# Moving the softmax exponential one slot later on ScalarE, in a fused attention and mixture-of-experts kernel

## The chip, the cores and the metric

The kernel runs on one core of a Trainium2 chip, in one launch. The metric is device time in microseconds (us): the median of three runs, and for the trace one profiled execution with its own time.

## The reference, cut to what matters

For 16 graphs of 512 nodes with 256 features, a masked attention with 8 heads of 32 is followed by a gate, and then by a mixture of 8 experts, top 2, with one shared expert. The change touches only the attention's softmax:

```python
q = (x @ Wq.T).reshape(b, n, NH, DK)          # b = 16, n = 512, NH = 8, DK = 32
k = (x @ Wk.T).reshape(b, n, NH, DK)
v = (x @ Wv.T).reshape(b, n, NH, DK)
scores = jnp.einsum('bqhd,bkhd->bhqk', q, k) / jnp.sqrt(jnp.float32(DK))
scores = jnp.where((adj != 0)[:, None, :, :], scores, -jnp.inf)
attn = jax.nn.softmax(scores, axis=-1)
c = jnp.einsum('bhqk,bkhd->bqhd', attn, v).reshape(b, n, h)
gate = jax.nn.sigmoid(jnp.concatenate([c, x], axis=2) @ Wg.T + bg)
return gate * x + (1.0 - gate) * c
```

x is layer-normalised before it, and the expert part comes after it on the sum of x and this result.

## The kernel before, in words

**Slots.** A batch is one graph. Its 8 heads times 4 tiles of 128 queries are 32 tiles of scores, each 128 x 512, and each tile has a slot p = 0 to 31 of the batch. Every engine walks the slots in the same order, written out in the program for all batches; the engines meet only at semaphores. A tile goes through a pipeline, and each step lags the score by a fixed number of slots, the constants at lines 82 to 86:

- TensorE in slot p: the score of tile p (L480); then four transposes of tile p - 3 (`TURN = 3`, L490), which first wait for the exponential of that tile (`p_exp`, L486) and for the copy of tile p - 5, whose PSUM bank they reuse (`t_free`, L488); then the slot's unit of other work; then, in slots 4, 12, 20 and 28, the product of P and V for 8 tiles (L511, 32 matmuls).
- VectorE in slot p: adds the mask to score p, scales, writes it to `pf` in SBUF and takes the row extreme `nmax` (L836, `s_done`); then the parts that belong to units.
- ScalarE in slot p: first it evacuates the unit that TensorE finished in slot p - 1 (L540 to L559); then it copies the transposed tile p - 4 out of PSUM (`EVAC = 4`, L597, `t_free`); then it takes the exponential of tile p - 1 (`EXP = 1`, L609), in place in `pf` with the row sums as accumulator output, which needs `s_done` of tile p - 1 and gives `p_exp`. Each exponential is two instructions, the ACTIVATE and the read of the accumulator. The copy is ahead of the exponential in each slot.

`pf` is a ring of 8 tiles, the scores have two PSUM banks, and the transposed tiles two.

**Units.** `UNIT_AT` (L24) puts the other work of a batch in slots: projections for the next batch (Q0 in slots 22 and 23, K0 in 24 and 25), for this one (Q1, K1, V0, V1 in 2 to 9), transposes (P0, P1, C0, C1, X0, X1), the gate (Z0 to Z3 in 14 to 17) and the router (L0, M0, R0 in 0, 1 and 12). A unit reaches VectorE for the low half after ScalarE has evacuated its high half.

**Head loads.** The query and key rows of a head are restacked by three DMAs from `qk` to `stack` (L303). SyncE issues those of heads 0 to 3 of the next batch, 12 in a row, once VectorE has the low half of K0 (L700). Score p of slots 0 to 3 needs head p there.

**Scatter.** From slot 17 GpSimd sends 8 indirect DMAs (L923) of the batch before to the experts' buffer.

After the 16th batch the engines pass to the experts' part (L1320 and on), of which only the beginning overlaps the attention.

Of the kernel before, what the change touches and what calls it, by code (L numbers as in the profile page):

```python
# [65 lines left out]
def attention_phase(nc, sems, held, banks, x, adj, wqkv, wgate, bg, router_w, xn_dram, x1_dram, xt2_dram, xg_dram,  # L66
# [13 lines left out]
    SCALE = float(DK) ** -0.5  # L80
    E = router_w.shape[1]
    TURN = 3
    EXP = 1
    EVAC = 4
    PV = 12
    BACK = 21
# [6 lines left out]
    if True:  # L93
# [187 lines left out]
        def behind(b, p, lag, att):  # L281

            if p >= lag:
                return b, p - lag, att
            before = att if not isinstance(b, int) else 0 < b <= NB
            return b - 1, p - lag + POS, before
# [239 lines left out]
        def scalar(act):  # L526
# [40 lines left out]
            def at(b, p):  # L567
# [22 lines left out]
                if was:  # L590
# [3 lines left out]
                    if ep % TB_ == 0 and (not isinstance(eb, int) or eb > 0 or ep >= 16):  # L594
# [4 lines left out]
                                   ACT.Copy).then_inc(t_free, 1)  # L599
                eb, ep, was = behind(b, p, EXP, att)  # L600
                if was:
# [1092 lines left out]
def program(nc, x, adj, wqkv, wgate, bg, router_w, w_all, out):  # L1694
# [12 lines left out]
    with ExitStack() as ctx:  # L1707
# [11 lines left out]
        with ExitStack() as held:  # L1719
            att = attention_phase(nc, ctx, held, banks, x, adj, wqkv, wgate, bg, router_w, xn_dram, x1_dram, xt2_dram,  # L1720
                                  xg_dram, ident, msum, xn2, idx, s_scat, region)
# [85 lines left out]
```

## Time and profile before

| | |
|---|---|
| median of 3 runs | 1925.34 us (1923.04 to 1927.98) |
| profiled execution, its own time | 1923.95 us |
| its span, first to last instruction | 1922.2 us |
| TensorE busy over the span | 1765.3 us (92%) |
| VectorE busy | 1274.3 us (66%) |
| ScalarE busy | 1104.5 us (57%) |
| 512 exponentials (L609), without the accumulator reads | 371.8 us |
| 512 copies of transposed tiles (L597) | 304.9 us |
| chain that ended last, share by engine | PE 42%, issue 1%, DMA 1% |

Times are read from the span's start. PE is TensorE's matmul side, PEld its weight loads (which the same sequencer issues, and which overlap the matmuls), DVE is VectorE, ACT is ScalarE, POOL is GpSimd, SP is SyncE. Idle time before an instruction is put down to what ended it. The clock column gives the granted TensorE clock as a share of full speed. The chain that ended last is traced only from 1034 us on, so that for the attention the timelines are read instead.

### The profile page before, as it was taken

How to read it: one execution, taken by the hardware profiler on the slowest of the kernel's cores; microseconds unless marked ns; L12 is line 12 of the kernel's file. 1: busy time of each engine (PE TensorE's matmuls, PEld its weight loads, DVE VectorE, ACT ScalarE, POOL GpSimd, SP SyncE). 2: the span in 40 equal slices, each digit the busy share in tenths (PEclk: the TensorE clock that was granted, in tenths of full speed). 3: DMA queues.
4: the chain of work that ended last, by engine and by line, in shares of the span. 5: the costliest groups of instructions: out<-in, count | busy, mean ns of one | idle time of the engine just before them, and what ended most of it. 6: DMA issues, size and time to landing. Idle time of an engine off the chain costs nothing. (4 is left out here: it accounts for less than half of the span.)

```text
span 1922.2 us, 36029 instructions
## 1 busy us (share of the span) xinstructions
PE 1765.3 (92%) x12613; PEld 1468.7 (76%) x12613; DVE 1274.3 (66%) x3155; ACT 1104.5 (57%) x2509; POOL 672.8 (35%) x512
## 2 busy tenths in 40 slices
PE   5899999988999888999889996989999999999996
PEld 4677777667777667777577885878989898898986
DVE  5676666766767766766645552467777777777773
ACT  4888778877778877778623331324444444444342
POOL 0125534335534335443221133003434343443334
PEclk8999999999999999999889996999999999999999
DMA  5445455544455544455213343245656565555553
GB/s 151 133 135 143 130 165 158 151 133 136 133 168 156 148 142 128 138 166 165 100 56 121 104 148 113 90 157 150 174 144 168 148 176 144 166 154 163 156 154 39
DMA packets 141329, 269.19 MB, mean 140 GB/s; under 512 B 15456, under 2 KB 92640, under 8 KB 136160
## 3 DMA queue, kind: packets, MB, share of 16 engines
q1 hardware_dynamic: 112608, 226.19, 38.3%
q0 software_dynamic: 28128, 39.93, 9.8%
q8 instruction: 102, 1.67, 0.4%
q10 hardware_dynamic: 416, 0.79, 0.2%
q14 instruction: 75, 0.61, 0.1%
HBM read 141.99 MB, written 74.52 MB: 113 GB/s over the span
## 5 line engine op out<-in xcount | busy, mean ns | idle before, releaser
L836 DVE CUSTOM_DVE_ANT_0 pf<-bank,bias_q 128x512 f32<-128x512 f32 x512 | 348.3, 687 | 268.6 <-PE bank L480 238.5
L1196 POOL DMA_INDIRECT out_x<-yb,ix x142 | 245.5, 1729 | 498.8 <-ACT yb L1414 408.0
L609 ACT ACTIVATE pf<-pf,nmax 128x512 f32<-128x512 f32 x512 | 371.8, 726 | 49.5 <-DVE nmax L836 49.5
L1426 ACT ACTIVATE ah<-am 128x512 fp32r<-128x512 f32 (+1 forms) x220 | 133.1, 605 | 440.8 <-DVE am L1494 434.8
L490 PE MATMUL bank<-ident,pf 128*128 128x128 f32 x2048 | 315.1, 276 | 55.5 <-issue 29.2
L1327 PE MATMUL bank<-xh,wl 128*128 128x512 f32 (+1 forms) x880 | 336.1, 382 | 6.0 <-issue 6.0
L490 PEld LDWEIGHTS bank<-ident,pf 128*128 128x128 f32 x2048 | 252.6, 142 | 115.3 <-issue 68.2
L1325 PE MATMUL bank<-xh,wh 128*128 128x512 f32 (+1 forms) x880 | 337.6, 384 | 3.2 <-issue 2.3
L1326 PE MATMUL bank<-xl,wh 128*128 128x512 f32 (+1 forms) x880 | 336.0, 382 | 2.0 <-issue 1.9
L597 ACT ACTIVATE pt<-bank 128x512 f32<-128x512 f32 x512 | 304.9, 596 | 13.9 <-PE bank L490 13.8
L480 PE MATMUL bank<-stack 96*128 96x512 f32 x512 | 237.2, 464 | 35.2 <-DMA stack<-qk 18.0
L1497 DVE TENSOR_TENSOR al<-am,ah 128x512 fp32r<-128x512 f32 (+1 forms) x220 | 146.7, 667 | 147.6 <-ACT ah L1426 144.8
L1325 PE MATMUL bank<-wh,ah 128*128 128x256 f32 x824 | 236.3, 287 | 3.5 <-issue 3.5
L1327 PE MATMUL bank<-wh,al 128*128 128x256 f32 x824 | 233.6, 283 | 3.6 <-issue 3.5
L1326 PE MATMUL bank<-wl,ah 128*128 128x256 f32 x824 | 233.2, 283 | 1.7 <-issue 1.7
L1494 DVE TENSOR_TENSOR am<-sg,bank 128x512 f32<-128x512 f32 (+1 forms) x220 | 143.0, 650 | 110.1 <-PE bank L1327 104.3
L1327 PEld LDWEIGHTS bank<-xh,wl 128*128 128x128 f32 x880 | 167.2, 190 | 39.3 <-issue 6.4
L1325 PEld LDWEIGHTS bank<-xh,wh 128*128 128x128 f32 x880 | 167.6, 190 | 38.3 <-issue 8.0
L1424 ACT ACTIVATE sg<-bank 128x512 f32<-128x512 f32 (+1 forms) x220 | 124.5, 566 | 121.0 <-PE bank L1327 88.8
L1326 PEld LDWEIGHTS bank<-xl,wh 128*128 128x128 f32 x880 | 167.7, 191 | 33.1 <-issue 2.6
L923 POOL DMA_INDIRECT xg_dram<-xn,idx x128 | 129.6, 1012 | 119.5 <-DVE idx L820 76.6
L480 PEld LDWEIGHTS bank<-stack 96*128 96x128 f32 x512 | 98.0, 192 | 88.8 <-issue 36.7
(213 smaller groups left out, 3202.3 us busy)
## 6 DMA issues: line engine op xcount, KB each, us to landing
raw<-in_w_all SPq DMA_DIRECT2D x39, 1536.0 KB, 7.3
stack<-qk SPq DMA_DIRECT2D x378, 128.0 KB, 2.4
xb<-xg_dram SPq DMA_DIRECT2D x32, 520.0 KB
adj_i<-in_adj SPq DMA_DIRECT2D x32, 512.0 KB, 5.1
xn<-in_x SPq DMA_DIRECT2D x16, 512.0 KB, 6.3
xn_dram<-xn SPq DMA_DIRECT2D x16, 512.0 KB
xp<-in_x SPq DMA_DIRECT2D x16, 512.0 KB, 6.7
xnp<-xn_dram SPq DMA_DIRECT2D x16, 512.0 KB, 7.6
```

The costliest lines, as they stand in the source:

```text
L480: pe.matmul(S[p % 2][:, :], stack[0:SR, hd, 0, P * tq:P * tq + P], stack[0:SR, hd, 1, :], start=True, stop=True).then_inc(s_full, 1)
L490: last = pe.transpose(T[ep % 2][:, P * kt:P * kt + P], pf[ep % RING][:, P * kt:P * kt + P], ident[:, :])
L597: act.activation(pt[r][:, j, :, P * (tq % 2):P * (tq % 2) + P], T[ep % 2][:, :].rearrange("p (k q) -> p k q", q=P), ACT.Copy).then_inc(t_f ...
L609: act.activation(pf[i][:, :], pf[i][:, :], ACT.Exp, bias=nmax[:, i:i + 1], scale=-1.0, accum_out=den[:, g, tq, j:j + 1]).then_inc(p_exp, 1)
L836: dve.tensor_tensor_reduce(pf[r][:, :], S[p % 2][:, :], bias_q[1 - par][:, tq, :], -SCALE, -3.0 * MASKED, ALU.add, ALU.min, nmax[:, r:r + ...
L1196: pool.indirect_dma_start(out=out, out_offset=bass.IndirectOffsetOnAxis(ap=ix[n % RING][:, i:i + 1], axis=0), in_=yb[s][:, i, :], in_offse ...
L1325: pe.matmul(out_, lh, rh, start=first, stop=False)
L1326: pe.matmul(out_, lh, rl, start=False, stop=False)
L1327: return pe.matmul(out_, ll, rh, start=False, stop=last)
L1426: act.activation(ah[s][:, m, 0:cols], am[m % 2][:, 0:cols], ACT.Copy).then_inc(s_ah, 1)
L1494: dve.tensor_tensor(am[m % 2][:, 0:cols], sg[m % 2][:, 0:cols], UB[m % 2][:, 0:cols], ALU.mult).then_inc(s_am, 1)
L1497: dve.tensor_tensor(al[s][:, m, 0:cols], am[m % 2][:, 0:cols], f32(ah[s][:, m, 0:cols]), ALU.subtract).then_inc(s_al, 1)
```

## The change

ScalarE takes the exponential of tile p - 2 in slot p, in place of that of tile p - 1. Nothing else is moved: the copy keeps its lag of 4, the transposes theirs of 3. The number of instructions and their sizes stay as they are; the last exponential of a batch now falls in slot 1 of the next one.

```diff
@@ -80,7 +80,7 @@
     SCALE = float(DK) ** -0.5
     E = router_w.shape[1]
     TURN = 3
-    EXP = 1
+    EXP = 2
     EVAC = 4
     PV = 12
     BACK = 21
```

## Rows read from the trace of the kernel before

**Rows 1.** Windows, attention: busy PE, PEld, DVE, ACT, POOL; clock, DMA share, GB/s

```profile
26.00:950.00 924.00, 834.99 (x7059) 650.23 (x7059) 633.27 (x1999) 736.72 (x1797) 364.38 (x292) 0.97 0.50 143
```

**Rows 2.** Waits, 240 to 890 us: who waited for whom, us, times, longest

```profile
ACT pf L609 <- DVE nmax L836: 26.6, 43, 1.2
...
PE bank L490 <- ACT pt L597: 18.8, 45, 0.7
...
PEld bank L480 <- DMA stack<-qk: 11.8, 17, 1.4
...
PE bank L480 <- DMA stack<-qk: 6.0, 11, 1.0
```

**Rows 3.** Timeline of ScalarE, slots 24 to 30: start, us, instruction, idle before

```profile
522.56 0.20 ACT L609 ACTIVATION_READ_ACCUMULATOR pf<-pf,nmax 128x1 f32 x1
...
523.50 0.73 ACT L609 ACTIVATE pf<-pf,nmax 128x512 f32<-128x512 f32 x1 [0.25 <-DVE nmax L836]
...
524.23 0.57 ACT L546 ACTIVATE qk<-bank 128x512 fp32r<-128x512 f32 x1
...
525.88 0.59 ACT L597 ACTIVATE pt<-bank 128x512 f32<-128x512 f32 x1
...
526.97 0.20 ACT L609 ACTIVATION_READ_ACCUMULATOR pf<-pf,nmax 128x1 f32 x1
...
530.01 0.60 ACT L597 ACTIVATE pt<-bank 128x512 f32<-128x512 f32 x1 [0.46 <-PE bank L490]
```

**Rows 4.** Timeline of TensorE's weight loads, slots 25 and 28

```profile
522.18 0.57 PEld L490 LDWEIGHTS bank<-ident,pf 128*128 128x128 f32 x4
...
526.59 0.42 PEld L490 LDWEIGHTS bank<-ident,pf 128*128 128x128 f32 x4 [0.61 <-ACT pf L609]
```

**Rows 5.** Timeline of TensorE's weight loads, slots 0 to 2 of the next batch

```profile
532.07 0.57 PEld L490 LDWEIGHTS bank<-ident,pf 128*128 128x128 f32 x4
...
534.80 0.47 PEld L490 LDWEIGHTS bank<-ident,pf 128*128 128x128 f32 x4
```

**Rows 6.** Timeline of ScalarE, slots 31 to 1

```profile
532.30 0.19 ACT L609 ACTIVATION_READ_ACCUMULATOR pf<-pf,nmax 128x1 f32 x1
...
533.92 0.28 ACT L556 ACTIVATE lgt<-bank 128x128 f32<-128x128 f32 x1 [0.24 <-PE bank L452]
...
535.18 0.20 ACT L609 ACTIVATION_READ_ACCUMULATOR pf<-pf,nmax 128x1 f32 x1
```

**Rows 7.** Timeline of TensorE: K0's last matmul in slot 25, z matmuls in slot 0

```profile
523.29 0.40 PE L396 MATMUL bank<-xt_h,wqkv_l 128*128 128x512 f32 x1
...
533.43 0.43 PE L452 MATMUL bank<-z,rw_wide 128*32 128x128 f32 x8 [0.20 <-DVE z L713]
```

**Rows 8.** Timeline of SyncE's queue: the loads of heads 0 to 3

```profile
526.53 7.98 SPq L303 DMA_DIRECT2D stack<-qk  x12
```

**Rows 9.** Timeline of ScalarE, slot 10

```profile
550.45 0.73 ACT L609 ACTIVATE pf<-pf,nmax 128x512 f32<-128x512 f32 x1 [1.22 <-DVE nmax L836]
```

**Rows 10.** Timeline of TensorE's weight loads, slots 11 and 12

```profile
550.47 0.19 PEld L480 LDWEIGHTS bank<-stack 96*128 96x128 f32 x1 [0.78 <-DVE nmax L836]
...
551.58 0.19 PEld L480 LDWEIGHTS bank<-stack 96*128 96x128 f32 x1
552.35 0.42 PEld L490 LDWEIGHTS bank<-ident,pf 128*128 128x128 f32 x4 [0.58 <-issue]
```

**Rows 11.** Timeline of TensorE, slots 20 and 28

```profile
512.72 0.63 PE L490 MATMUL bank<-ident,pf 128*128 128x128 f32 x4 [2.52 <-issue]
513.27 3.62 PE L511 MATMUL bank<-pt,v 128*32 128x256 f32 x32
...
527.17 1.93 PE L511 MATMUL bank<-pt,v 128*32 128x256 f32 x32
```

**Rows 12.** Timeline of GpSimd's scatter, the last of 8 DMAs

```profile
512.04 0.96 POOL L923 DMA_INDIRECT xg_dram<-xn,idx  x1 [0.30 <-issue]
```

**Rows 13.** Windows, the product of slot 20: columns as in the first group

```profile
514.00:516.00 2.00, 2.00 (x24) 1.05 (x20) 1.38 (x4) 1.60 (x4) 0.00 (x0) 0.50 0.00 0
```

## The prediction, made before the change was run

> **What bounds the kernel now.** I began with the busy time by stretch. In the 924 us of attention TensorE is busy 835 us and ScalarE 737 us [rows 1]: near enough that each paces some slots. The table of waits says where they meet: ScalarE's exponentials wait for VectorE 43 times, 26.6 us in all, which is what the change goes for; and TensorE's transposes wait for ScalarE's copies 45 times, 18.8 us, which is what it may worsen [rows 2]. The chain of waits does not reach back to the attention, so I then went through the timelines of one batch (500 to 558 us) slot by slot; the other batches repeat it to some hundredths, except in slots 0 to 3 and at both ends.
>
> The key reading is the distance between a copy on ScalarE and the transposes that reuse its bank. The copy that starts at 525.88 ends at 526.47, and the next transposes' weight load starts at 526.59, 0.12 us later [rows 3, 4]. TensorE stands there and goes as soon as the copy is out. (The page names L609 as releaser; that exponential had long been done, it is the copy.)
>
> **What the change does to the order.** Transposes of slot p need the exponential of tile p - 3. Before, ScalarE takes it in its slot p - 2; with the change it is the last thing of slot p - 1, behind the very copy that TensorE already waits for. No instruction is added. The wait of TensorE in slot p is now for the end of ScalarE's slot p - 1. The exponential that stands there in the trace tells when: its accumulator read ends at 526.97 + 0.20 = 527.17, so the load that started at 526.59 starts at 527.28 or later, 0.69 us late [rows 3, 4]. What was queued behind it on TensorE is the unit of the slot, or the product of P and V, then the next score, for which VectorE waits.
>
> In the other direction ScalarE gains: its 43 waits for `nmax` go, since that tile is a slot older.
>
> **Where the delay counts.** Only where ScalarE or VectorE later wait for TensorE.
>
> *Slots 25 to 29.* ScalarE is the pacer from 524.23 on, without a gap, to 529.5. In slot 25 the transposes start at 522.18, and ScalarE's slot before ends at 522.76; plus 0.11 that is 0.69 late. K0's last matmul, which ends at 523.69 now, then ends at 524.38, and K0's evacuation, at 524.23 now, follows at about 524.4: +0.2. ScalarE's wait of 0.25 in that slot vanishes, but the evacuation is then held by TensorE, so the gain is not kept [rows 3, 4, 7]. Then ScalarE runs its slots at its own pace, and the transposes of slot 28 come 0.69 + 0.2 = 0.89 late. Behind them is the product of P and V, 1.93 us [rows 11], after which TensorE is the pacer: ScalarE's copy in slot 30 waits 0.46 us for it already [rows 3]. So the whole 0.89 us lands on ScalarE.
>
> *Slot 0.* The transposes start at 532.07, ScalarE's slot ends at 532.49, plus 0.11: 0.53 late, on top. Then come the z matmuls, of which the second half waits 0.20 us for VectorE, which absorbs that much; the evacuation of L0 already waits 0.24 us for them. Net +0.34 [rows 5 to 7].
>
> *Slot 2.* Start 534.80, ScalarE's end 535.38, plus 0.11: 0.69, call it 0.70 late, ahead of Q1 and the score of slot 3 [rows 5, 6]. Sum from slot 25 to slot 3: 0.89 + 0.34 + 0.70 = 1.93 us.
>
> *What absorbs part of it.* The score of slot 3 waits for head 3's load. The 12 loads leave SyncE's queue one after the other in 7.98 us from the low half of K0 on [rows 8], so they shift only by about 0.2 us, and TensorE, coming later, waits less. Over the twelve batches from 240 us these waits total 6.0 us on the matmul side and 11.8 us on the load side [rows 2]: 0.50 to 0.98 us a batch. I take 0.70, since a part of a load's wait is the ordinary spacing. Net 1.93 - 0.70 = 1.23 us a batch, 14.8 us in twelve. The three seams before them have longer waits for the loads, so I give them 2.0 us together.
>
> *Slots 7 to 11.* Transposes 0.0 to 0.2 us late, but VectorE paces here: the score of slot 11 waits for it, 0.78 us at the load [rows 10]. Cover is enough; uncovered it would be 0.2 us a batch, 3 us.
>
> *Slot 12, the gain.* ScalarE waits 1.22 us for `nmax` in slot 10 [rows 9], and for that reason its slot 11 copy is late and the transposes of slot 12 wait 0.58 us. That load starts at 552.35, so the copy ended at about 552.24; ScalarE's slot 11, exponential included, ends 0.70 us after its copy, and without the wait 1.22 us sooner: 551.7, before TensorE comes. TensorE is then held by its own order only. Of the 0.77 us from the score's load to the transposes' (551.58 to 552.35), the load itself takes 0.19 and the wait 0.58; some 0.2 of idle stays at a score ahead of transposes, so about 0.39 us is gained [rows 10], at most 0.39 x 13 = 5.1 us. I take it as nothing for all batches with a scatter: TensorE stands in slots 18 to 20 while the 8 scatter DMAs go out (2.52 us before the transposes of slot 20; last issue 512.04) [rows 11, 12], and the scatter hangs on VectorE's variance in slot 12, which is not moved. It comes to the same stretch a little earlier and waits more.
>
> *Slots 19 and 20.* Both transposes would be 0.69 late, but in the same stand. I take nothing, and keep 0.69 x 12 = 8.3 us as the upper bound. Slots 14 to 18 are paced by the gate's matmuls; nothing.
>
> *First batches.* No scatter yet: two product slots come late, two gain in slot 12: +0.3 us.
>
> *The end.* The experts' part starts behind the last batch and is passed on whole.
>
> **Sum.** 14.8 + 2.0 + 0.3 = 17.1 us. Against the profiled execution's own 1923.95 us (span 1922.2) that is 1941.0; that execution is 1.4 us under the median of the runs, so 1941 to 1942.4. I predict 1941, 0.8% slower. Downward: the full gain of slot 12 (-5.1) and the larger absorption (-0.28 x 12 = -3.4): 1932.5. Upward: the smaller absorption (+2.4) and slots 19 and 20 (+8.3): 1951.7.
>
> **The clock.** Slot 20's product runs at a granted clock of 0.50 (1.2 of 2.4 GHz) after the stand of 2.52 us, and takes 3.62 us, where that of slot 28 takes 1.93 us [rows 11, 13]. The change widens the wait ahead of the transposes of slot 28 from 0.61 to some 1.3 us, and that of slot 27 likewise. Should the clock fall there as well, each batch pays up to 3.62 - 1.93 = 1.69 us more. In this batch only the longer stand was followed by a fall, so this is a rival and no term. The Trainium skill, "TensorE: Matmul & The Clock Gate", Part 1 ("The HAM clock gate") says that an idle TensorE is throttled to half its clock and activity releases it, and Part 4 ("PE-mode transpose") that transposes do not count as activity in the same way, which speaks against a change that leaves little but transposes and waits there. By that rule the time would be that of the clock rival below; by the row of slot 28's product, 1.93 us behind a wait of 0.61 us and transposes, it is not [rows 4, 11].
>
> **The rivals.**
> - *Slower, as summed:* 1941, own range 1932 to 1952. Chance 0.80 (with slots 19 and 20 in it).
> - *Hidden:* the head loads are the real pacer of each seam, and the transposes' delay only eats into their wait. Each seam then costs the 0.2 us of K0: 15 x 0.2 = 3 us, 1927. It decides where the wait for loads is above 1.9 us in each batch; the longest is 1.4 [rows 2]. Chance 0.10.
> - *Faster:* ScalarE freed of its 26.6 us of waits runs ahead, and its earlier copies let TensorE start the slots after 10 sooner: 15 x 0.39 = 5.9 us, 1918. It needs ScalarE's slot to end before TensorE comes in slots 25, 0 and 2 too, where it now ends 0.4 to 0.6 us after. Chance 0.05.
> - *Clock:* 1941 + 14 x 1.69 = 1965. Chance 0.05.
>
> A measurement of this kernel tells about 0.3% (6 us) from no change. Faster by more: 0.04; within: 0.11; slower: 0.85. Range for eight times in ten: 1931 to 1952.
>
> **What the profile after would show.** Right: the transposes' wait for L609 or the issue in slots 2, 12 (smaller), 19, 20, 25, 27 and 28, each load starting 0.11 us behind an accumulator read and not behind a copy; the exponentials' waits for `nmax` nearly gone; slots 29 to 29 of the next batch 58 to 60 us apart, with nearly no wait for `stack`; slots 14 to 18 unchanged. Wrong: a granted clock of 0.5 near slot 28 (clock); the load wait still there in slot 3 (hidden); slots 12 to 21 shorter by 0.4 us (gain kept) or longer (slots 19 and 20 count). The weakest steps are the stand in slots 18 to 20, which I take as given from outside without knowing its cause, and the mean of 0.70 for the head loads.

## The result, and the profile after

The changed kernel took 1941.93 us in the median of 11 runs (1934.48 to 1948.19), the kernel before 1925.61 us in 11 runs beside it (1923.04 to 1932.9). The ratio is 1.0074, with a 95% interval of 1.0057 to 1.0091: slower by 0.74%. Its profiled execution took 1940.37 us with a span of 1938.6 us; before these were 1923.95 and 1922.2.

The groups of instructions on the page after, with busy time, mean ns of one, and idle time before them:

```profile
L836 DVE CUSTOM_DVE_ANT_0 pf<-bank,bias_q 128x512 f32<-128x512 f32 x512 | 349.0, 687 | 280.5 <-PE bank L480 251.2
...
L490 PE MATMUL bank<-ident,pf 128*128 128x128 f32 x2048 | 323.4, 281 | 74.9 <-ACT pf L609 40.3
...
L609 ACT ACTIVATE pf<-pf,nmax 128x512 f32<-128x512 f32 x512 | 371.3, 725 | 9.4 <-DVE nmax L836 9.4
L490 PEld LDWEIGHTS bank<-ident,pf 128*128 128x128 f32 x2048 | 250.1, 143 | 149.8 <-ACT pf L609 78.4
...
L597 ACT ACTIVATE pt<-bank 128x512 f32<-128x512 f32 x512 | 305.0, 596 | 37.6 <-PE bank L490 37.3
```

The exponentials hardly wait any more (9.4 us left in the whole span, 49.5 us before). In their place the transposes' weight loads stand 78.4 us behind the exponential, and ScalarE's copies stand 37.3 us behind TensorE (13.8 us before). No instruction became slower: 725 ns for an exponential, 596 ns for a copy. The waits of the same stretch as [rows 2], 240 to 890 us (who waited for whom, us in all, times, longest):

```profile
PEld bank L490 <- ACT pf L609: 51.1, 70, 1.3
...
PE bank L490 <- ACT pf L609: 26.6, 56, 1.0
...
ACT qk L546 <- PE bank L396: 24.3, 44, 0.9
ACT pt L597 <- PE bank L490: 23.5, 29, 1.1
...
PE bank L490 <- ACT pt L597: 4.9, 3, 1.8
...
PEld bank L480 <- DMA stack<-qk: 3.4, 8, 0.7
```

The wait that the change goes for, ScalarE's for `nmax` (43 times before), is gone from the list; that of the transposes for the copies fell from 45 times to 3; and the loads' wait for the heads' DMAs fell from 11.8 to 3.4 us, since TensorE comes later. The first row is what grew. Before the change it read:

```profile
PEld bank L490 <- ACT pf L609: 7.3, 12, 0.6
```

One seam, batch 9 into batch 10, with ScalarE in slots 24 to 30 and then 0 to 2, to be laid beside [rows 3, 6]:

```profile
591.19 0.60 ACT L546 ACTIVATE qk<-bank 128x512 fp32r<-128x512 f32 x1 [0.25 <-PE bank L396]
...
592.78 0.20 ACT L609 ACTIVATION_READ_ACCUMULATOR pf<-pf,nmax 128x1 f32 x1
...
593.96 0.20 ACT L609 ACTIVATION_READ_ACCUMULATOR pf<-pf,nmax 128x1 f32 x1
...
597.64 0.60 ACT L597 ACTIVATE pt<-bank 128x512 f32<-128x512 f32 x1 [1.10 <-PE bank L490]
...
602.82 0.20 ACT L609 ACTIVATION_READ_ACCUMULATOR pf<-pf,nmax 128x1 f32 x1
```

And TensorE's weight loads in the same stretch, to be laid beside [rows 4, 5]: slots 25, 27 and 28, then 0, the z matmuls, and 2; the last two are the score's and the transposes' of slot 12, to be laid beside [rows 10].

```profile
589.81 0.42 PEld L490 LDWEIGHTS bank<-ident,pf 128*128 128x128 f32 x4 [0.70 <-ACT pf L609]
...
593.03 0.42 PEld L490 LDWEIGHTS bank<-ident,pf 128*128 128x128 f32 x4 [1.28 <-ACT pf L609]
...
594.22 0.42 PEld L490 LDWEIGHTS bank<-ident,pf 128*128 128x128 f32 x4 [0.61 <-ACT pf L609]
...
600.17 0.42 PEld L490 LDWEIGHTS bank<-ident,pf 128*128 128x128 f32 x4 [0.42 <-ACT pf L609]
600.76 0.46 PEld L452 LDWEIGHTS bank<-z,rw_wide 128*32 128x32 f32 x16 [0.17 <-issue]
...
603.07 0.42 PEld L490 LDWEIGHTS bank<-ident,pf 128*128 128x128 f32 x4 [0.69 <-ACT pf L609]
...
619.37 0.19 PEld L480 LDWEIGHTS bank<-stack 96*128 96x128 f32 x1
619.62 0.46 PEld L490 LDWEIGHTS bank<-ident,pf 128*128 128x128 f32 x4
```

Read the two together. The accumulator read that starts at 592.78 ends at 592.98, and the load goes at 593.03; the next ends at 594.16, the load goes at 594.22; the one of slot 1 ends at 603.02, the load of slot 2 goes at 603.07. Each load goes 0.05 or 0.06 us behind the end of ScalarE's whole slot, where before it went 0.12 us behind the copy [rows 3, 4]. In slot 12 the transposes' load follows the score's after 0.25 us without a wait, where it took 0.77.

**Where the 16.4 us of span went.** The start of each score (L480) marks the slots. I took its distance from the score before over batches 3 to 14, and give the means in us:

| slots | before | after | |
|---|---|---|---|
| 0 to 5 | 9.62 | 9.56 | -0.06 |
| 5 to 12 | 10.43 | 10.42 | 0 |
| 12 to 13 | 3.53 | 3.05 | -0.48 |
| 13 to 18 | 9.61 | 9.62 | 0 |
| 18 to 21 | 9.53 | 10.15 | +0.62 |
| 21 to 24 | 4.06 | 4.27 | +0.21 |
| 24 to 29 | 8.32 | 8.90 | +0.58 |
| 29 to 0 | 2.92 | 2.92 | 0 |
| batch | 58.02 | 58.88 | +0.86 |

Twelve batches make 10.36 us (12 x 0.863). Up to the first score of batch 3 it is 186.83 - 183.36 = 3.47 us, in the last batch 1.36 us, behind its last score 1.23 us; the sum is 16.42 us. Of the 3.47 us, 2.6 lie in batch 0, and 0.94 lie ahead of the very first score (at 26.97 us after, 26.03 before), where no exponential has run yet: that part is not the change's. The first score starts at 25.1 to 27.0 us in all the kernels of this document.

### The profile page after: what moved, and what is told of

It is laid out like the page before. It is cut to its first block and busy times, and to the rows that moved or that the text cites. A ratio compares the mean times of both kernels' runs of the same rounds, so it can differ in the third digit from the quotient of the medians.

```text
span 1938.6 us, 36029 instructions
## 1 busy us (share of the span) xinstructions
PE 1772.6 (91%) x12613; PEld 1469.6 (76%) x12613; DVE 1281.5 (66%) x3155; ACT 1105.2 (57%) x2509; POOL 672.0 (35%) x512
## 5 line engine op out<-in xcount | busy, mean ns | idle before, releaser
L490 PE MATMUL bank<-ident,pf 128*128 128x128 f32 x2048 | 323.4, 281 | 74.9 <-ACT pf L609 40.3
L609 ACT ACTIVATE pf<-pf,nmax 128x512 f32<-128x512 f32 x512 | 371.3, 725 | 9.4 <-DVE nmax L836 9.4
L490 PEld LDWEIGHTS bank<-ident,pf 128*128 128x128 f32 x2048 | 250.1, 143 | 149.8 <-ACT pf L609 78.4
L597 ACT ACTIVATE pt<-bank 128x512 f32<-128x512 f32 x512 | 305.0, 596 | 37.6 <-PE bank L490 37.3
L480 PE MATMUL bank<-stack 96*128 96x512 f32 x512 | 235.5, 460 | 26.4 <-DVE nmax L836 11.5
L1325 PEld LDWEIGHTS bank<-wh,ah 128*128 128x128 f32 x824 | 156.1, 189 | 6.1 <-issue 5.6
```

Of the source, the lines that this page charges most:

```text
L480: pe.matmul(S[p % 2][:, :], stack[0:SR, hd, 0, P * tq:P * tq + P], stack[0:SR, hd, 1, :], start=True, stop=True).then_inc(s_full, 1)
L490: last = pe.transpose(T[ep % 2][:, P * kt:P * kt + P], pf[ep % RING][:, P * kt:P * kt + P], ident[:, :])
L597: act.activation(pt[r][:, j, :, P * (tq % 2):P * (tq % 2) + P], T[ep % 2][:, :].rearrange("p (k q) -> p k q", q=P), ACT.Copy).then_inc(t_f ...
L609: act.activation(pf[i][:, :], pf[i][:, :], ACT.Exp, bias=nmax[:, i:i + 1], scale=-1.0, accum_out=den[:, g, tq, j:j + 1]).then_inc(p_exp, 1)
L1325: pe.matmul(out_, lh, rh, start=first, stop=False)
```

## The experiments

Every kernel here computes all that the kernel before does. The kernel before was timed again beside each.

**Order against lag (two runs).** In both, ScalarE's exponential stands ahead of its copy in each slot; the first keeps the old lag, the second takes the new one.

```diff
-                eb, ep, was = behind(b, p, EVAC, att)
...
                 eb, ep, was = behind(b, p, EXP, att)
...
+                eb, ep, was = behind(b, p, EVAC, att)
```

> The exponential keeps its lag of one slot, but stands ahead of the copy in ScalarE's slot. Theory (what costs is that the transposes wait for the end of ScalarE's previous slot, whichever instruction stands there): the transposes of slots 25, 27, 28, 2, 19 and 20 start 0.11 us behind the end of a copy that now stands last, some 0.5 to 0.7 us later than before, and slots 24 to 29 take about 8.9 us in place of 8.26. The waits for nmax stay (26.6 us between 240 and 890 us). Time 1935 to 1950 us. Rival (the greater age of the exponential is what costs, the order in a slot is nothing): 1925 us, slots 24 to 29 at 8.26.

> The exponential two slots behind, as in the changed kernel, and ahead of the copy. Theory (end of the slot counts): the two orders are alike, since the transposes need both the exponential and the copy of the same slot of ScalarE; slots 24 to 29 at 8.8 to 8.9 us, time 1937 to 1946 us. Rival (it is the exponential's place behind the copy that costs): the transposes' waits fall back to the 0.61 us of before, 1925 us or below, since the waits for nmax are gone too.

Lag 1: 1947.55 us, ratio 1.0109 (1.0087 to 1.0132). Lag 2: 1945.21 us, ratio 1.0102 (1.0082 to 1.0121). Both times are in the ranges expected; slots 24 to 29 are somewhat longer than expected, 9.38 us with lag 1 and 9.03 with lag 2. With lag 2 the transposes wait for a copy that now ends ScalarE's slot, and the product of slot 28 starts 7.17 us behind the score of slot 24, as against 7.03 after the change and 6.39 before. So it doesn't matter much which of the two instructions is last: TensorE needs both, and what costs is that it needs the end of the slot. (This order is, if anything, some 0.3% slower than the change; the two intervals overlap a little.) With lag 1 the exponential's wait for `nmax` also holds the copy behind it, which is the other way to lose. Slots 5 to 12 take 11.53 us there, before 10.43. ScalarE in the exponential-first kernel with lag 1, in slots 29 and 30:

```profile
597.28 0.60 ACT L608 ACTIVATE pt<-bank 128x512 f32<-128x512 f32 x1
599.53 0.72 ACT L598 ACTIVATE pf<-pf,nmax 128x512 f32<-128x512 f32 x1 [1.64 <-DVE nmax L836]
600.16 0.19 ACT L598 ACTIVATION_READ_ACCUMULATOR pf<-pf,nmax 128x1 f32 x1
600.25 0.57 ACT L608 ACTIVATE pt<-bank 128x512 f32<-128x512 f32 x1
```

**All of the pipeline one slot later.** If the cost is only that TensorE needs the end of ScalarE's slot, then moving the transposes, the copies and the product too should leave the gain alone.

```diff
-    TURN = 3
-    EXP = 1
-    EVAC = 4
-    PV = 12
-    BACK = 21
+    TURN = 4
+    EXP = 2
+    EVAC = 5
+    PV = 13
+    BACK = 22
```

(`SEAM_HEAD`, the number of slots at a batch's head that still belong to the batch before, goes from 4 to 6.)

> Exponential, transposes, copy, product and the evacuation of the product all one slot later (2, 4, 5, 13, 22), and the first expert step two slots later so that the last tiles are out of its banks. Theory: the distance from exponential to transposes is back, so no transposes wait for an accumulator read; slots 24 to 29 at 8.26 us or near, slots 0 to 3 back to a floor of 4.10, and the gain of slot 12 (0.4 to 0.5 us a batch) is kept or lost in the stand of slots 18 to 20. 1918 to 1927 us. Rival (the later exponentials cost in another way, through the masked scores' ring or the row sums): 1935 us or more.

It took 1968.78 us, ratio 1.0208 (1.0185 to 1.0232): a plain miss. The products land in slots 5, 13, 21 and 29, beside other units than before, and a batch takes 61.15 us: slots 21 to 24, with the product of slot 21 among them, take 11.08 us (before 4.06), while slots 18 to 21 take 5.71 (before 9.53). That is not the stall of slots 18 to 20 moving away. TensorE in slots 20 and 21 of batch 9 of that kernel:

```profile
590.13 0.63 PE L490 MATMUL bank<-ident,pf 128*128 128x128 f32 x4 [2.53 <-issue]
590.51 0.48 PE L480 MATMUL bank<-stack 96*128 96x512 f32 x1
593.07 1.09 PE L490 MATMUL bank<-ident,pf 128*128 128x128 f32 x4 [2.08 <-ACT pt L597]
594.09 3.64 PE L511 MATMUL bank<-pt,v 128*32 128x256 f32 x32
```

It stands 2.53 us in slot 20, as before (2.52), and then another 2.08 us in slot 21. ScalarE shows why: its evacuations of P0 and P1 come late here as they do before (idle 2.04 and 1.16 us ahead of them, before 2.04 and 1.14), but before, the product of slot 20 runs while the second is late and covers it. With the product one slot on, the second stand is bare, and the product behind it still takes 3.64 us. Slots 18 to 24 take 16.79 us, before 13.59: 3.20 us a batch, or 38 of the 42 us lost. The run says nothing for or against the reason under test, as it changes what stands beside what.

**The delays taken back one group at a time.** A constant `LATE` lists the tiles whose exponential comes two slots behind; the others keep one. A tile's transposes follow in the third slot behind it.

```diff
-    EXP = 1
+    LATE = (8, 9, 10)
...
-                eb, ep, was = behind(b, p, EXP, att)
-                if was:
+                for lag in (2, 1):
+                    eb, ep, was = behind(b, p, lag, att)
+                    if not was or (ep in LATE) != (lag == 2):
+                        continue
```

Those are the tiles of the gain in slot 12 alone. The other three keep lag 2 for all tiles but those whose transposes fall in slots 24 to 29, in slots 31 to 2, or in slots 18 to 21.

> Only the exponentials of tiles 8, 9 and 10 of each batch are taken two slots behind, all others one. Theory: slot 12's transposes no longer wait, slots 12 to 13 take about 3.05 us in place of 3.53, no other stretch but the stand of slots 18 to 21 is touched. If the stand swallows it, 1925 us; if it is kept, 1925.6 - 0.48 x 13 = 1919 us. I expect it to be swallowed: 1923 to 1926.

> As the changed kernel (two behind), but tiles 21 to 26 of each batch, whose transposes fall in slots 24 to 29, one behind as before. Theory: slots 24 to 29 fall from 8.90 back to 8.3 us, the floor of slots 0 to 3 stays at 4.68, slots 12 to 13 stay at 3.05; 0.6 x 15 = 9 us less than the changed kernel, 1933 us, if the stand of slots 18 to 21 is as in the changed kernel. Rival (the loss of the changed kernel is in the stand alone): 1942 us.

> As the changed kernel, but tiles 28 to 31 of each batch, whose transposes fall in slots 31 to 2, one behind as before. Theory (the head loads absorb what is late here): the floor of slots 0 to 3 falls from 4.68 to 4.10 us, and the waits for the loads come back, so that the mean of slots 0 to 3 stays near 4.5 to 4.8; the time moves by -4 us at most, 1938 to 1942. Rival (the loads absorb nothing): -0.58 x 15 = -9 us, 1933.

> As the changed kernel, but tiles 15 to 18 of each batch, whose transposes fall in slots 18 to 21, one behind as before. Theory A (the stand got 0.8 us longer because its transposes are dispatched later): slots 18 to 24 fall from 14.4 to about 13.6 us and the time to 1931. Theory B (it got longer because TensorE comes to it 0.48 us earlier relative to the scatter): they stay at 14.4 or scatter from batch to batch as now, 1940 to 1943. In batches 0 and 1, which have no scatter, slots 18 to 21 lose 0.3 to 0.6 us in both.

| late tiles | us | ratio (interval) | slots 0-3 | 12-13 | 18-24 | 24-29 | batch |
|---|---|---|---|---|---|---|---|
| none (before) | 1925.6 | 1 | 4.82 | 3.53 | 13.59 | 8.32 | 58.02 |
| all (after) | 1941.93 | 1.0074 (1.0057 to 1.0091) | 4.80 | 3.05 | 14.42 | 8.90 | 58.88 |
| 8 to 10 | 1924.45 | 0.9994 (0.9982 to 1.0007) | 4.91 | 3.05 | 13.16 | 8.55 | 57.49 |
| not for 24 to 29 | 1935.99 | 1.0038 (1.0015 to 1.0060) | 5.03 | 3.05 | 14.20 | 8.18 | 58.20 |
| not for 31 to 2 | 1937.86 | 1.0057 (1.0034 to 1.0080) | 4.70 | 3.05 | 14.65 | 8.90 | 59.06 |
| not for 18 to 21 | 1931.74 | 1.0027 (1.0013 to 1.0041) | 4.77 | 3.05 | 14.05 | 8.90 | 58.48 |

The slot columns are means of batches 3 to 14 in one profiled execution. Three things follow.

First, slots 24 to 29: with the old lag there they are back at 8.18, from 8.90, and the time falls by 0.36% (1.0074 to 1.0038; the two intervals just overlap). It was this delay that lengthened them. But the waits for the heads come back, 4.80 to 5.03 in slots 0 to 3. Second, slots 31 to 2: taking the delay back there gives 0.10 us in slots 0 to 3 and a fall of the ratio by 0.17%, which its interval doesn't tell from nothing. The head loads had absorbed that delay. Third, slots 18 to 21: taking the delay back there gives 0.47%, 1.0074 to 1.0027. The two intervals don't meet. (That it gives more than slots 24 to 29 do is not shown.) Its trace shows less of it than its time: slots 18 to 24 take 14.05 us, which is 0.37 less than after the change and 0.46 more than before, but its profiled execution was the slowest of its ten (1936.67 us).

The gain of slot 12 by itself is there in every batch, 3.53 to 3.05 us, but with it alone the time is 0.9994 of that before, which is no measured gain: 12 x 0.48 = 5.8 us would be 0.30%, and the interval ends at 0.18%. So at least part of it is lost again behind slot 12. The profiled execution of that kernel was the fastest of its 12 (1916.04 us), so its batch of 57.49 us flatters it.

**The stall in slots 18 to 20.** I had taken it as given, without its cause. In the next runs the scatter's 8 DMAs are held until VectorE is in slot 20 of the batch, with lag 1, with lag 2, and with the three late tiles; in the last they are let go one per slot from slot 17 on, with lag 1.

```diff
+                    if A + 2 < NB:
+                        pool.wait_ge(s_done, (A + 2) * POS + 20)
```

```diff
+                if A + 2 < NB:
+                    pool.wait_ge(s_done, (A + 2) * POS + 17 + j)
```

> The kernel before (exponentials one behind), with GpSimd's scatter held until the score of slot 19 is masked, some 5 us later than it would start. Theory (the stand is tied to the scatter, not to the slots): P0 and P1 are evacuated 1.66 and 3.3 us after the score of slot 18, as in batch 1, slots 18 to 21 take 5.3 to 6 us, and a stand appears in slots 21 to 26 in their place; its sum decides the time, 1900 to 1935. Rival (the stand belongs to slots 18 to 20, scatter or not): slots 18 to 21 stay at 9.5 us, 1925.

> All exponentials two behind, with the scatter held until the score of slot 19 is masked, to be read against the same with one behind (1925 us). Slots 18 to 21 are then free of the stand in both. Theory (late transposes in slots 19 and 20 cost when no stand covers them): slots 18 to 21 take 5.31 + 0.65 = 5.95 us, slots 12 to 13 3.05 in place of 3.53, the floor of slots 0 to 3 4.7 in place of 4.1, and in slots 24 to 29, where the stand now is, from nothing to 0.64 more. Sum per batch -0.48 + 0.65 + 0.58 + (0 to 0.64) = 0.75 to 1.4 us, 1935 to 1944 us. Rival (the changed kernel is slow only because its stand is longer): 1925 us or below.

> Tiles 8 to 10 two behind, the rest one, and the scatter held as in the run before with one behind. Theory (the gain of slot 12 is kept, since the scatter now hangs on the score of slot 19, which comes earlier too): slots 12 to 13 at 3.05, nothing else changed, 1925 - 0.48 x 14 = 1918 us. Rival (what is gained ahead of the scatter is given back in its stand wherever it is): 1925 us.

> The kernel before, with the eight scatter DMAs of a batch sent one per slot, held until the scores of slots 16 to 23 are masked, in place of one after the other. Theory A (the stand is caused by each DMA, or by the bytes): its sum is the same, spread over slots 18 to 26, 1925 us. Theory B (it comes from their following each other closely): slots 18 to 21 fall to 5.3 to 6 us and the later ones stay, up to 4.3 x 12 = 50 us less, 1875 us. Slots with transposes and late evacuations show which.

Held, with lag 1: 1924.92 us, ratio 0.9985 (0.9971 to 1.0). Slots 18 to 21 fall from 9.53 to 5.31 us, and slots 24 to 29 rise from 8.32 to 13.44: the stall went with the scatter, at full size, and so gained nothing. GpSimd's DMA issues of that kernel in batch 9, the second and the last:

```profile
573.75 1.92 POOL L925 DMA_INDIRECT xg_dram<-xn,idx  x1 [0.30 <-issue]
...
582.33 0.96 POOL L925 DMA_INDIRECT xg_dram<-xn,idx  x1 [0.30 <-issue]
```

TensorE, from K0's last matmul in slot 25 on (the second line is the score of slot 27, the third the transposes of slot 27, the last the product of slot 28):

```profile
580.71 0.40 PE L396 MATMUL bank<-xt_h,wqkv_l 128*128 128x512 f32 x1
...
581.62 0.48 PE L480 MATMUL bank<-stack 96*128 96x512 f32 x1
585.81 1.09 PE L490 MATMUL bank<-ident,pf 128*128 128x128 f32 x4 [3.70 <-ACT pt L597]
...
588.11 3.59 PE L511 MATMUL bank<-pt,v 128*32 128x256 f32 x32
```

and ScalarE's evacuation of that K0:

```profile
584.58 0.60 ACT L546 ACTIVATE qk<-bank 128x512 fp32r<-128x512 f32 x1 [2.85 <-remote]
```

Read the three in order of time. The last DMA issue ends at 583.29. K0's last matmul had ended at 581.11, and ScalarE had nothing else to do from 581.73 on, yet it begins K0's evacuation at 584.58, 3.5 us behind the matmul; its wait is put down to no instruction ("remote"). The copy behind it comes late, and so TensorE stands 3.70 us. The product then takes 3.59 us, much as that of slot 20 does before [rows 11]; the half clock costs 3.59 - 1.93 = 1.66 us, and moves with the stall.

The three others ran on another chip, where the kernel before takes 1836.92 us in 13 runs (1833.02 to 1841.12), 4.6% less than on the chips of all runs above. They can be compared with that time only. Held, lag 2: 1870.09 us, ratio 1.0177 (1.0155 to 1.02). Held, three tiles late: 1872.0 us, 1.0187 (1.0161 to 1.0213). Spread, lag 1: 1841.08 us, 1.0021 (1.0009 to 1.0033).

| kernel | 0-3 | 12-13 | 18-21 | 24-29 | 29-31 | batch |
|---|---|---|---|---|---|---|
| held, all tiles late | 4.68 | 3.05 | 5.95 | 8.90 | 3.76 | 55.71 |
| held, three tiles late | 4.22 | 3.05 | 5.31 | 8.28 | 5.74 | 56.33 |
| spread, no tile late | 4.68 | 3.53 | 5.31 | 8.28 | 2.45 | 53.80 |

None of the three has the stall, though the two held ones send their 8 DMAs as closely as the first held kernel did, which had it at full size. In the spread kernel of that table TensorE's transposes and product of slot 20 go like this, though DMAs of the scatter are issued at 540.93, 542.20 and 544.04 us:

```profile
542.23 0.63 PE L490 MATMUL bank<-ident,pf 128*128 128x128 f32 x4 [0.27 <-ACT pt L597]
542.79 1.93 PE L511 MATMUL bank<-pt,v 128*32 128x256 f32 x32
```

Here the change's own terms can be read without it: +0.64 in slots 18 to 21 (5.95 against 5.31), +0.62 in slots 24 to 29, -0.48 in slot 12. What the two held kernels lose is something else: the transposes of the next batch's rows (slots 29 and 30) wait for GpSimd, which normalises them behind the held scatter. The waits of the held kernel with all tiles late, 240 to 890 us:

```profile
PE bank L400 <- POOL xn L966: 14.5, 11, 1.6
```

In the held kernel on the other chip slots 29 to 31 take 2.24 us as before; there the stall ahead of them seems to give GpSimd the time.

The profile of the kernel before was not taken on the faster chip, so that it has no stall there is argued, but on good grounds. Its time is 4.6% less, and the spread kernel, whose time is within 0.3% of it, has none in its trace. And the experts' part, which is the same code in all kernels, has a second train of indirect DMAs, 32 in a row from L1178 (a line or two later in some kernels). The 60 us from the first of them on, in the columns of [rows 1], first in the kernel before and then in the spread kernel:

```profile
1132.00:1192.00 60.00, 42.16 (x186) 33.05 (x185) 19.63 (x42) 11.81 (x20) 31.80 (x32) 0.74 0.43 141
```

```profile
1075.00:1135.00 60.00, 60.00 (x333) 52.24 (x332) 31.59 (x60) 20.97 (x35) 32.02 (x32) 1.00 0.60 194
```

TensorE stands 17.6 us around them in the first, at a mean clock of 0.74, and not at all in the second. It is so in every trace: 17.6 to 22.4 us in the eleven of the slower chips, none in the three of the faster one. From the first of these DMAs to the end of the span it is 790.2 to 794.3 us there and 764.3 to 765.0 here. Since the train is not spread in the spread kernel either, it is the chip that makes this difference. Whether spreading the scatter would remove the stall on the other chips stays open.

One kernel had lost most of the stall already, on a slower chip and with the scatter untouched: the exponential ahead of the copy, lag 1. Its slots 18 to 21 take 6.01 us in eight batches of the twelve (before 9.5 to 9.8 in eleven). TensorE's P0 and ScalarE's evacuation of it, first before, then in batch 9 of that kernel:

```profile
507.73 0.60 PE L400 MATMUL bank<-ident,xn 128*128 128x128 f32 x4
...
511.49 0.60 ACT L540 ACTIVATE xt_h<-bank 128x512 fp32r<-128x512 f32 x1 [2.04 <-remote]
```

```profile
578.20 0.60 PE L400 MATMUL bank<-ident,xn 128*128 128x128 f32 x4
...
579.19 0.60 ACT L540 ACTIVATE xt_h<-bank 128x512 fp32r<-128x512 f32 x1
...
581.67 1.93 PE L511 MATMUL bank<-pt,v 128*32 128x256 f32 x32
```

The evacuation starts 3.16 us behind the matmuls before, and 0.39 us behind them here, and the product of slot 20 (the last line) runs at full speed. Yet the scatter is issued around all of this, from 573.15 to 584.74 us. So the scatter beside these slots is not enough for the stall. What the order of ScalarE's two instructions has to do with it, no run tells. The kernel is still slower than before, by what its exponentials' waits cost elsewhere (slots 5 to 12 +1.10 us, 24 to 29 +1.06, 29 to 0 +0.36).

**The change once more.** The last run was the changed kernel itself.

> The changed kernel itself, once more, in the hope of a chip on which the kernel before takes 1837 us. The kernel before took 1926 to 1927 us on two chips and 1837 us on a third. My theory: what the change costs by its order (0.64 us in slots 25 to 29, 0.58 us in slots 0 to 2 less 0.59 us that the head loads absorb, 0.48 us won in slot 12) is the same on each chip, and what happens in slots 18 to 24 is not. Where the kernel before takes about 1926 us I expect a ratio of 1.007 again and slots 18 to 21 at 9.5 to 10.5 us. Where it takes about 1837 us I expect slots 18 to 21 at 5.3 to 6.0 us, slots 24 to 29 at 8.90, and 14 to 20 us more than before, 1.008 to 1.011. Rival, that the cost is mostly the stand's: there no more than 6 us, 1.003.

It fell on a chip where the kernel before takes 1927.04 us: 1940.45 us (1938.02 to 1945.27), ratio 1.0078 (1.0063 to 1.0094), with slots 18 to 21 at 10.11 us, 24 to 29 at 8.90 and slot 12 at 3.05. The result was got a second time, and the question it was sent for was not answered.

## Why the prediction was right, and where it was not

The time, 1941 forecast and 1941.93 measured, and the main mechanism are right: the transposes wait for the end of ScalarE's slot, the exponentials' waits are gone, and much of the cost is at the seams. But that the sum came out within 1 us is partly luck: errors of 4.4 and 3.8 us cancel.

*Slots 25 to 29.* Predicted 0.89 us, measured 0.64. Before, the product of slot 28 starts 6.39 to 6.41 us behind the score of slot 24 in ten batches of the twelve (6.75 and 6.79 in the other two); after, 7.03 or 7.04 in all. The 0.2 us for K0's evacuation was not there: it starts 3.42 to 3.45 us behind that score both before and after, apart from two batches at 3.8. K0's last matmul had ended 0.54 us ahead of the evacuation [rows 3, 7], and that slack took nearly all of a delay that was itself 0.06 us shorter than reckoned, as the load goes 0.05 us behind the accumulator read and not 0.11.

*Slot 0.* Predicted +0.34, measured none: the first two scores are 1.82 us apart after and 1.83 before. The z matmuls, which ran as two trains of 8 with a wait for VectorE between [rows 7], run as one train of 16 after. Their weight loads are in the fence above. The later start took up all of the wait and the idle time around it.

*Slot 2.* Predicted 0.70; the shortest stretch from score 0 to score 3, without a wait for a head, went from 4.10 to 4.68: 0.58.

*The head loads.* Predicted to absorb 0.70 a batch. The mean wait above that floor was 4.82 - 4.10 = 0.72 before and is 4.80 - 4.68 = 0.12 after: 0.60 absorbed, so the whole of slots 0 to 3 costs nothing. The kernel with the old lag for slots 31 to 2 confirms it: the stretch stays at 4.70.

*Slot 12.* Predicted 0.39 us sooner, measured 0.48, in every batch. That it would vanish in the stall was the step taken with least reason, and the runs bear it out in the main: alone it brought no time, and the scatter, which starts 0.15 us into TensorE's slot 16 before, starts 0.57 us into it after, as TensorE comes earlier to the same stall. Slots 18 to 24 took 0.83 us more, so of the two together 0.35 us were lost, and not nothing.

*Slots 19 and 20.* Here is the mis-sized term. I took nothing and kept 8.3 us as an upper bound. The run with the old lag for those slots won back 0.47%, 9 us, and where there is no stall they cost 0.64 us a batch, 12 x 0.64 = 7.7. So a delay was not hidden by the stall, it came on top. How the 0.83 us divide is not sharp: by the trace with the old lag there, 0.46 are the swallowed gain of slot 12 and 0.37 the delay; by its time the delay is more. The price of 0.64 is read from the kernels without a stall; in those with it, single batches of the change range from 8.7 to 11.25 us in slots 18 to 21, so that only the means carry it.

*First batches and end.* Predicted 2.3 us, measured 3.47 + 1.36 + 1.23 = 6.1, of which 0.94 lie ahead of the first score and are not the change's. Batch 0 alone lost 2.6 us: 0.70 ahead of slot 15, 0.64 in slots 15 to 18 (3.00 to 3.64), 1.00 in slots 24 to 29 (7.90 to 8.90), 0.49 in slot 31, less 0.25 won in slots 18 to 21. I had given it the cost of the later batches, though its slots carry other units.

So per batch 1.23 us were forecast and 0.86 measured (-4.4 us over twelve), and 3.8 us more stand at the ends, of which 0.9 lie ahead of the first score.

*The rivals.* "Hidden" fell: slots 0 to 3 did behave so, but slots 18 to 21 and 24 to 29 have no head load to hide behind. "Faster" fell with the 51.1 us of loads waiting for L609, 7.3 before. "Clock" fell: the loads of slots 27 and 28 wait 1.28 and 0.61 us, and the product behind them still takes 1.93 us. The mean granted clock was 0.966, before 0.968. TensorE in slots 20 and 28 after, to be laid beside [rows 11]:

```profile
579.74 1.02 PE L490 MATMUL bank<-ident,pf 128*128 128x128 f32 x4 [3.23 <-issue]
580.69 3.20 PE L511 MATMUL bank<-pt,v 128*32 128x256 f32 x32
...
594.80 1.93 PE L511 MATMUL bank<-pt,v 128*32 128x256 f32 x32
```

Waits up to 1.3 us among transposes cost no clock here; a stand of 2.52 us before, of 3.23 here and of 3.70 with the scatter held did. So did one of 1.80 to 1.84 us in slot 20, in five of the twelve batches after the change: the product behind it takes 2.79 to 3.14 us. Of the rule cited in the prediction (the Trainium skill, "TensorE: Matmul & The Clock Gate", Parts 1 and 4), the trace shows the half that an idle TensorE is throttled; that transposes don't hold the clock up, it does not show at waits of this length.

## What to carry to other kernels

When a step is moved later by a slot, ask what its consumer waited for before: if that was already an instruction of the same engine in the same slot, then the consumer will now wait for the end of the whole slot, and one exponential with its read (here 0.64 us) is added wherever that engine is the pacer. An average of idle time that the change removes (26.6 us of waits here) says nothing of the gain: only 0.48 us in one slot of 32 was won by it, and even that brought no measurable time. And a delay that runs into a stall of unknown cause is not to be counted as hidden; keep its full price in the sum until a run has shown otherwise.

## What the runs showed of the hardware

While the scatter's last DMAs go out, ScalarE begins an evacuation 3.2 us (before) to 3.5 us (scatter held) behind the matmul that it waited for, and TensorE stands next: 2.5 us before, 3.2 us after, 3.7 us with the scatter held. The stall goes where the scatter goes (9.53 to 5.31 us in one stretch, 8.32 to 13.44 in the other), so the scatter has a part in it. It is not enough by itself: with the exponential ahead of the copy and lag 1, eight batches of twelve go through slots 18 to 21 in 6.01 us beside the same scatter. By what path, that the matmul's signal came late or that ScalarE itself was held, no run told apart; a kernel without the scatter wasn't tried.

The kernel before takes 1925.6 to 1927.0 us in four groups of runs, and 1836.92 us in a fifth, on a chip of its own. The three kernels profiled on that chip show no stall, and else the same durations: 3.05 us for slot 12 and 8.90 for slots 24 to 29 with the new lag, to the hundredth. The experts' part differs too: behind the last score it is 979.2 to 986.5 us on the slower chips and 953.7 to 957.4 on this one, and nearly all of that comes at and behind the 32 indirect DMAs of L1178, where TensorE stands 17.6 us or more on the slower chips and not at all here. So on both sides it is what TensorE stands beside trains of indirect DMAs that tells the chips apart, as far as traces were taken.

With the change the runs also spread more, 1934.48 to 1948.19 us (0.7%) as against 1923.04 to 1932.9 (0.5%). Slots 18 to 24, the ones with the stall, are the only ones after the change that vary by more than 0.5 us from batch to batch (slots 18 to 21: 8.73 to 11.25).
